# Row maxima stacked under the queries, one ring of four PSUM banks, and one exponential per slot in a vision-transformer block

## The reference

```
gray  = einsum('bchw,c->bhw', x, (0.2989, 0.587, 0.114))
h     = (|conv(gray, scharr_x)| + |conv(gray, scharr_y)|) / 2      # (8, 256, 256): 256 tokens of 256
n     = layernorm(h)
q,k,v = n@Wq+bq, n@Wk+bk, n@Wv+bv        # 16 heads of 16
q,k   = q@Wp, k@Wp                       # per head, 16 x 16
out   = softmax(q k^T / 4) v             # per head, 256 queries by 256 keys
h     = h + out
n2    = layernorm(h)
h     = h + ffn(n2)   # its own layernorm, 256 -> 1024 (silu) -> 256 with dequantised weights, residual + 0.5 z
```

## Time and profile before

| what | value |
|---|---|
| median of 3 runs | 294.59 us |
| the profiled execution | 294.29 us, span 292.6 us, so 1.7 us lie around the span |
| PE busy | 279.8 us (96%), 2336 matmuls |
| DVE busy | 205.7 us (70%) |
| ACT busy | 173.2 us (59%) |
| POOL busy | 145.2 us (50%) |
| mean granted clock of PE | 0.994 |
| DMA packets | 35.9 MB |

### The profile page before, as it was taken

How to read it: one execution, slowest core, us unless ns; L and a number is a source line. 1 busy time by engine, 2 the same in 40 slices (tenths; PEclk the granted TensorE clock), 3 DMA queues, 4 the chain that set the end, 5 groups by cost and what they waited for, 6 DMA issues and landing times.

```text
span 292.6 us, 6337 instructions
## 1 busy us (share of the span) xinstructions
PE 279.8 (96%) x2336; PEld 217.2 (74%) x2336; DVE 205.7 (70%) x394; ACT 173.2 (59%) x330; POOL 145.2 (50%) x286
## 2 busy tenths in 40 slices
PE   4989799999998999999999999999999999999996
PEld 4876678686876676666666665658898999999985
DVE  7659887589988888888998886717926724632323
ACT  2457979766324877777768786686353344444450
POOL 7894387311100129592768655086589399400000
PEclk9999799999999999999999999999999999999999
DMA  6968649998979915676660000000002000100202
GB/s 201 312 193 239 172 165 269 191 275 259 314 217 329 297 43 164 184 208 218 192 157 3 0 2 3 0 3 0 2 0 67 8 0 16 60 0 0 74 0 72
DMA packets 27310, 35.90 MB, mean 123 GB/s; under 512 B 5184, under 2 KB 16272, under 8 KB 27280
## 3 DMA queue, kind: packets, MB, share of 16 engines
q1 hardware_dynamic: 27184, 35.43, 41.4%
q10 hardware_dynamic: 96, 0.07, 0.1%
HBM read 24.42 MB, written 10.49 MB: 119 GB/s over the span
## 4 chain that ended last, share of the span: by engine, by line
PE 70%; DVE 9%; ACT 6%; issue 5%; POOL 4%; DMA 3%; ACTq 1%; SPq 1%; DVEq 0%; POOLq 0%
PE bank L1227 35%; PE bank L1355 9%; PE bank L1307 9%; PE bank L1330 5%; PE bank L1335 4%; DVE negmax L925 4%; PE bank L1373 3%; DMA halo_x<-in_x 2%; PE bank L1365 2%; PE bank L1244 2%; PE bank L1381 1%; ACTq L401 1%; ACT absd L1104 1%; ACT hid L1101 1%; POOL rstd L639 1%
## 5 line engine op out<-in xcount | busy, mean ns | idle before, releaser
L925 DVE TENSOR_REDUCE negmax<-bank 128x2 f32<-128x512 f32 x128 | 82.0, 683 | 6.9 <-PE bank L1307 6.5
L1137 ACT ACTIVATE probs<-bank 128x512 f32<-128x512 f32 x128 | 66.3, 602 | 30.5 <-PE bank L1335 30.5
L979 DVE TENSOR_TENSOR y_l<-yf,y_h 128x512 fp32r<-128x512 f32 x32 | 24.2, 755 | 38.6 <-ACT yf L1163 38.4
L1160 ACT ACTIVATE y_h<-bank,b1col 128x512 fp32r<-128x512 f32 x32 | 22.0, 689 | 47.7 <-PE bank L1227 47.6
L1227 PE MATMUL bank<-w_h,y_h 128*128 128x256 f32 x128 | 36.8, 288 | 0.4 <-DVE osb L987 0.4
L1227 PE MATMUL bank<-w_l,y_h 128*128 128x256 f32 x128 | 36.2, 282 | 0.0
L1227 PE MATMUL bank<-w_h,y_l 128*128 128x256 f32 x128 | 36.1, 282 | 0.0
L1355 PE MATMUL bank<-probs,vals 128*32 128x256 f32 x512 | 34.3, 385 | 0.0
L1307 PE MATMUL bank<-ks,qs 48*128 48x256 f32 x256 | 32.1, 328 | 1.8 <-DVE negmax L925 0.9
L1307 PEld LDWEIGHTS bank<-ks,qs 48*128 48x128 f32 x256 | 19.3, 184 | 15.9 <-DVE negmax L925 7.6
L1330 PE MATMUL bank<-negrow,pick 48*128 48x512 f32 x128 | 26.1, 403 | 0.6 <-DVE pick L1026 0.6
(11 more groups left out here) (164 smaller groups left out, 600.3 us busy)
## 6 DMA issues: line engine op xcount, KB each, us to landing
xr<-in_x SPq DMA_DIRECT2D x8, 768.0 KB, 7.9
qs<-qk_parts SPq DMA_DIRECT2D x48, 128.0 KB, 3.2
ks<-qk_parts SPq DMA_DIRECT2D x48, 128.0 KB, 3.3
qk_parts<-qk_h SPq DMA_DIRECT2D x16, 256.0 KB, 3.1
qk_parts<-qk_l SPq DMA_DIRECT2D x16, 256.0 KB, 3.4
wraw<-in_L_ffn_fc_q SPq DMA_DIRECT2D x4, 512.0 KB, 4.7
wscale<-in_L_ffn_fc_scales SPq DMA_DIRECT2D x4, 512.0 KB, 7.3
out<-osb SPq DMA_DIRECT2D x16, 128.0 KB, 1.8
```

Of the source, the lines that this page charges most:

```text
L925: eng.tensor_reduce(negmax[:, b % 2, u, v], entry_bank(key)[:, :].rearrange("p (t k) -> p t k", t=NT), AX.X, ALU.max, negate=True).then_in ...
L979: eng.tensor_tensor(y_l[:, p % 2, f], yf[:, n % 2], y_h[:, p % 2, f].bitcast(fp32), ALU.subtract).then_inc(s_y, 1)
L1137: eng.activation(probs[:, n % PBUF], p2[n % 4][:, :], ACT.Exp).then_inc(s_exp, 1)
L1160: eng.activation(y_h[:, p % 2, f], src, ACT.Silu, bias=b1col[:, f:f + 1])
```

## The change

1. **Maxima as rows of the stacks.** `STACK = SPLIT + 2` rows are contracted: two rows of `qs` hold the high and the low part of minus the maximum, the same two rows of `ks` hold ones. The matmuls of L1330, `pick` and `picked` go. `negrow` goes to DRAM (`store_max`) and comes back into `qs` by two DMAs (`load_max`), both on SP's queue. The ones are written by DMAs once.
2. **Layout of `qk_parts`**: high and low of a row lie next to each other, so that a half of a pair's stacks is loaded by 8 DMAs instead of 12; the bytes are the same.
3. **One ring of four banks** all through, with the value products as entries of it (`av`). The by-key scores have two buffers of two banks, and one exponential of 1024 columns takes a whole slot (`exp_slot`).
4. **Order**: `AHEAD` 12 instead of 10 (the scores of slots 10 and 11 now belong to the projections of the last pair, those of 8 and 9 stand one step earlier there, and slots 52 to 63 issue no by-query scores); `neg` behind slots 1 and 5 of each eight, `out` behind 3 and 7; so in the steady part every pair of slots has exactly one of the two. The second `neg` of image 0 moves ahead of the slots. GpSimd's weight steps start at slot 6 instead of 10, behind them the other steps at other slots; the second layer's raw weights are fetched at slots 20 and 21 instead of 23 and 24. `OBUF` 7, `PBUF` 12.

```diff
-    AHEAD = 10
+    AHEAD = 12
+    PARTS = 2
+    STACK = SPLIT + PARTS
...
-        NEG_AT = {("qkv", 2, 5): 0}
+        NEG_AT = {("qkv", 2, 5): 0, ("qkv", 3, 3): 1}
         def neg_after(s):
             b, i = s // UNITS, s % UNITS
-            if s == 1:
-                return (0, 1)
-            if i in (3, 7) and b + 1 < B:
+            if s >= 0 and i in (1, 5) and b + 1 < B:
                 return (b + 1, i // 4)
         def out_after(s):
             b, i = s // UNITS - 1, s % UNITS
-            if b >= 0 and i in ((3, 5) if b < B - 1 else (3, 4)):
-                return (b, i // 4 if b == B - 1 else (i - 3) // 2)
+            if b >= 0 and i in ((3, 7) if b < B - 1 else (3, 4)):
+                return (b, i // 4)
...
             if s + AHEAD < SLOTS:
                 head_entries(s + AHEAD)
+            if s % 2 == 1 and 0 <= s - 3 < 2 * GROUPS:
+                entries.append(("av", (s - 3) // 2))
...
             if n < wide:
-                r = n % 4 if n < in_a else n % 3
+                r = n % 4
+            elif key[0] == "av" or key[0] == "out" and key[1] == B - 1 or key[0] == "n3" and key[1] >= 1:
+                r = 0
             else:
-                r = 1 if key == ("n3", 0, 1) else 0
+                r = 1 if key == ("n3", 0, 1) else 3
...
+            def store_max(b, half):
+                eng.wait_ge(s_neg, 2 * b + half + 1)
+                eng.dma_start(neg_dram[b, half], negrow[0:MROWS, half].bitcast(fp32)).then_inc(s_negst[half], 16)
+            def load_max(b, half):
+                r, c = (b // 2) % 2, (b % 2) * N
+                eng.wait_ge(s_negst[half], 16 * (b + 1))
+                for v in range(2):
+                    first = HALF * v + SPLIT
+                    src = neg_dram[b, half, HALF * v:HALF * v + 4 * PARTS].rearrange("(a u) n -> a u n", a=PARTS)
+                    eng.dma_start(qs[first:first + PARTS, r, 4 * half:4 * half + 4, c:c + N].bitcast(fp32), src).then_inc(s_maxrow[half], 16)
...
-            for part in range(4):
+            for part in range(2):
                 load_ffn(0, part)
+            load_max(0, 1)
+            for part in range(2, 4):
+                load_ffn(0, part)
             for s in range(SLOTS):
+                if neg_after(s - 1):
+                    store_max(*neg_after(s - 1))
+                if neg_after(s - 3):
+                    load_max(*neg_after(s - 3))
...
-                if s % UNITS == 1 and b + 1 < B:
-                    split_max(b + 1, 0)
-                if s % UNITS == 5 and b + 1 < B:
-                    split_max(b + 1, 1)
+                if s % UNITS in (0, 4) and b + 1 < B:
+                    split_max(b + 1, s % UNITS // 4)
...
-            def exp_head(n):
+            def exp_slot(s):
...
-                eng.activation(probs[:, n % PBUF], p2[n % 4][:, :], ACT.Exp).then_inc(s_exp, 1)
+                eng.activation(probs[:, n % PBUF:n % PBUF + 2].rearrange("p v n -> p (v n)"), p2[s % 2][:].rearrange("p v n -> p (v n)"),
+                               ACT.Exp).then_inc(s_exp, 1)
...
             def scores_by_key(s):
...
                 if u % 4 == 0:
-                    wait_drained(eng, ("neg", b, u // 4))
+                    eng.wait_ge(s_maxrow[u // 4], 32 * (b + 1))
...
-                for v in range(2):
-                    rows = slice(HALF * v, HALF * v + SPLIT)
-                    eng.matmul(p2[(n + v) % 4][:, :].rearrange("p (t n) -> p t n", t=NT), pick[rows, u % 4:u % 4 + 1].broadcast_to([SPLIT, P]),
-                               negrow[rows, u // 4].unsqueeze(1).broadcast_to([SPLIT, NT, N]), start=True, stop=False)
                 for t in range(NT):
                     for v in range(2):
-                        rows = slice(HALF * v, HALF * v + SPLIT)
-                        ins = eng.matmul(p2[(n + v) % 4][:, t * N:(t + 1) * N], ks[rows, r, u, c + t * P:c + (t + 1) * P],
-                                         qs[rows, r, u, c:c + N], start=False, stop=t == NT - 1)
+                        rows = slice(HALF * v, HALF * v + STACK)
+                        ins = eng.matmul(p2[s % 2][:, v, t * N:(t + 1) * N], ks[rows, r, u, c + t * P:c + (t + 1) * P],
+                                         qs[rows, r, u, c:c + N], start=True, stop=True)
...
                     if G == 0:
                         eng.wait_ge(s_zero, 4)
...
-                    else:
-                        eng.wait_ge(s_ot, G)
+                    wait_room(eng, ("av", G))
```

More of the change, by code:

```diff
@@ L348, in vit_tower_kernel @@
             entries.extend(("n3", p, kf) for kf in range(KE))
-        entry = {key: n for n, key in enumerate(entries)}
-        assert len(entry) == len(entries)
-        drained = {key: n for n, key in enumerate(key for key in entries if key[0] != "neg")}
+        place = {key: n for n, key in enumerate(entries)}
+        assert len(place) == len(entries)
+        entry = {key: n for n, key in enumerate(key for key in entries if key[0] != "av")}
+        drained = {key: n for n, key in enumerate(key for key in entries if key[0] not in ("neg", "av"))}
         ebank, before, held = {}, {}, {}
@@ L372, in wait_drained @@
                 eng.wait_ge(s_neg, 2 * key[1] + key[2] + 1)
+            elif key[0] == "av":
+                eng.wait_ge(s_ot, key[1] + 1)
             else:
@@ L376, in wait_room @@
         def wait_room(eng, *keys):
-            used = sorted((before[key] for key in keys if before[key]), key=lambda key: entry[key])
-            for kind in (True, False):
-                last = [key for key in used if (key[0] == "neg") == kind][-1:]
+            used = sorted((before[key] for key in keys if before[key]), key=lambda key: place[key])
+            for kind in ("neg", "av", None):
+                last = [key for key in used if (key[0] if key[0] in ("neg", "av") else None) == kind][-1:]
                 if last:
@@ L434, in load_qk @@
                 dst = (qs, ks)[op]
-                first = HALF * v + slot
-                src = qk_dram[p, op, part, m * P:(m + 1) * P, :].rearrange("(u v d) t -> v d u t", v=2, d=D)[v]
-                eng.dma_start(dst[first:first + SPLIT - 2:3, r, m * 4:(m + 1) * 4, :].bitcast(fp32), src).then_inc(s_load[r][m], 16)
+                rows = qk_dram[p, op, m * P:(m + 1) * P]
+                if k // 2 % 2 == 0:
+                    first, last = HALF * v, HALF * v + 2 * D
+                    src = rows.rearrange("(u v d) a t -> v (d a) u t", v=2, d=D)[v]
+                else:
+                    first, last = HALF * v + 2 * D, HALF * v + 3 * D
+                    src = rows[:, 1 - op].rearrange("(u v d) t -> v d u t", v=2, d=D)[v]
@@ L487, in _ @@
                 stored(0, m)
-                for k in range(12):
+                for k in range(LOADS):
                     load_qk(0, m, k)
+            stack_ones(0)
             for i in range(4):
```

139 lines of the change are left out of this document (75 added, 64 removed).

## The result

The changed kernel takes **301.59 us** (median of 4 runs, 299.66 to 305.17) against 294.7 us of the kernel before on the same chip: ratio 1.021, 95% interval 1.0135 to 1.0293. It is slower; whether by more than 2% the interval leaves open. Medians here are of all executions, while ratios and their intervals leave out the slow ones, those over 1.5% above the fastest of their kernel (of these four, 305.17). The forecast was 291.4 us with a range of 286.0 to 296.0, so both the sign and the range were wrong. The profiled execution took 300.22 us, its span 298.5 us.

What follows compares the result with a forecast made beforehand. It took the refill loop between PE and VectorE through the four-bank ring as the bound, 3.16 us a pair. Last reduction at 175.0 and last value products at 193.7, 2.9 us earlier, gave 294.3 − 2.9 = 291.4 us, range 286.0 to 296.0.

Steps and rivals of the forecast that it cites:

- PE's load and the steady pair: Attention slots: PE loses 0.23 us in each of 64 slots; the refill loop sets a steady pair at 3.16 us.
- Rival A: Steady pairs: the refill loop does not bind, VectorE's own 2.83 us a pair does; 284.1 us, chance 0.17.
- C: Rival on ScalarE: exponentials of 1.2 us make its pairs 3.2 us and the tail 2.4 longer; 293.8 us, chance 0.11.
- What the change could gain: Slots: by PE's row alone 14.7 us; by the PSUM reading rule alone, only what VectorE idles now.
- Where the slots begin: Start of the slots: heads one step earlier, so slot 12's reductions begin about 1.6 us earlier, at 92.0.
- The maxima's way at the start: Slot 4, image 0: the load of maxima stands behind two 512 KB transfers; PE waits 1.5 us, bounds 0 and 4.7.
- In the steady part two DMAs fit into 11 us: Steady slots: seven slots, 11 us, lie between the maxima's transposition and use, so store and load fit.
- GpSimd's first weight step: Slot 6: it waits for the last weight transfer, ahead of the next maxima's split; 0.3 us, bounds 0 and 1.8.
- Loads two slots sooner: Stack loads: readers come two slots earlier, at least four slots (over 6 us) of cover remain; cost nothing.
- Rival B: SP's queue, image 0, slots 4 and 9: first maxima land late, 4.7 us more; 296.1 us, chance 0.13.
- Rival D: PE's idling lowers the clock to 0.83, its pairs become 3.4 us, 4.4 us more; 295.8 us, chance 0.05.
- Tail: From the last reduction to the start of the last value products: forecast 18.7 us, last value products at 193.7.

Runs made afterwards that it cites:

- e6: The changed kernel without maxima in any form, with the by-query scores refilling the ring by single banks instead of two together: 288.91 us, ratio 0.9792 to the kernel before.
- e4_before_no_max: The kernel before without the 128 matmuls of 512 columns that subtract the maxima; maxima still formed, transposed and copied: 292.6 us, ratio 0.9941.
- e5_no_rows: The changed kernel without the maxima in any form: 48 rows contracted, no rows of ones or maxima, none stored or loaded: 294.71 us, ratio 1.000 to the kernel before.
- e9_direct: The changed kernel with the maxima moved from negrow straight into qs by four 4 KB transfers, without the trip through DRAM: 296.74 us, 5 below the changed kernel.
- e13_early_plain: The changed kernel with direct maxima transfer, early stack loads, feed-forward weights at slots 24 and 25, GpSimd's w1 steps from slot 8: 291.64 us, ratio 0.990 to before.
- e7: The changed kernel with the maxima's store on ScalarE's queue, image 0's second load ahead of the weights, later second-matrix weights and w1 steps: 299.7 us, ratio 1.007 to before.

## Why the prediction was wrong

- *PE's load and the steady pair.* Right: 3.16 forecast, 3.08 to 3.14 measured, for the reason given (0.59 us idle or a division in its place). Rival A did not come, and even with e6's edit a pair takes 3.00, not 2.83. C did not come: the two exponentials of a pair take 1.94 us.
- *What the change could gain.* Right in size (before 13.24 an image, after 12.45). Taking the matmuls away alone brings none of it (e4_before_no_max); what is left to bring it is the ring's order and the division inside the refill. Whether that would come with the 512-wide matmuls kept was not tested: by the prediction's own terms PE would then need 3.04 + 0.46 = 3.50 us in every second pair, more than the 3.16 of the loop.
- *Where the slots begin.* Right: slot 12's heads begin at 91.9, forecast 92.0.
- *The maxima's way at the start.* The step that failed, first half. I gave 1.5 + 0.3 us with bounds 4.7 and 1.8. I placed the wait behind the weights of 512 KB and took SP's own progress from the kernel before. Not seen: `load_max(0, 0)`, placed three DMAs behind its store, holds SP 6.2 us, so that the second store, whose data were ready 9 us before, went out 3 us after the time I had for the first weights. Slot 4 then waited 3.35 us, not 1.5, and the stretch cost 4.6 us over the 12.6 forecast.
- *In the steady part two DMAs fit into 11 us.* The step that failed, second half. I set no duration against the 11 us, though the page had 7.3 us for a transfer in company. Stores of 72 KB took 5.9 and 7.2 us at image 3, in series with SP's order, and slots 39 to 43 took 10.4 us where two pairs were to take 6.3: 4.1 us. The Trainium skill ("DMA: Bandwidth & Descriptors", Anatomy of one DMA) has some 2 us fixed for one DMA issued by GpSimd; an estimate from that page would be 4 us for the two. That is a transfer by itself and of another issuer; the rows here are 3.2 to 7.9 us for the store behind others.
- *GpSimd's first weight step*: I put 0.3 us on it, bound 1.8. It waited 7.8 us in after, under slot 4's lateness. Without that cover a wait of 7.1 us cost some 4.5 (e5_no_rows: slots 19 to 31 in 23.2, at its own 6.22 for four slots 18.7), one of 4.8 us nothing (e9_direct).
- *Loads two slots sooner "cost nothing".* Wrong too, hidden in after: 3.1 us at head 36 when the maxima are punctual (e9_direct).
- *Rival B* named the right place and the right wait, slot 4's, but put it down to the weights ahead of the load; what made it late is the earlier load that held SP. It saw one image; that its 4.7 us are near the 4.6 of image 0 is luck. *Rival D*: in the steady pairs the clock stayed at 1.00 (120 to 130); it fell at the start, for some 1.4 us by e9_direct, and in other runs in the tail, for 1.2 to 1.4.
- *Tail.* 19.05 for 18.7.

Shown by runs: with the direct transfer, the early loads, the later weights and GpSimd's later step, and all else as in after, the kernel comes to the forecast (e13_early_plain). Of the 10 us between, leaving the trip out gives 7 (e5_no_rows), replacing it alone 5 (e9_direct). Open: how the 5 us between e9 and e13 divide between the early loads, the later weights and GpSimd's later step; and why the kernels with the new transfers vary by 3 to 9 us from run to run.

## What to carry to other kernels

An engine busy 99% need not be the bound; look whether the one behind it idles in a closed loop, and take the work away as a test. A new dependent transfer must be costed twice: from issue to landing in the company it will have, and as a wait that holds all that is queued behind it on its queue. When a wait disappears, see what it had covered: here the late maxima had covered GpSimd's wait for its weights and TensorE's wait for the stacks.

## What was not expected of the hardware

- A store of 72 KB took 3.2 to 7.9 us in after while the DMA share was about 1.0 (7.9 for the one issued at 79.39), and 5.5 from ScalarE's queue in e7; where the share was 0.16 it took 1.6 (112.04 to 113.64).
- Rows moved from four partitions to one inside SBUF by four DMAs of 4 KB took 2.4 us of SP's queue to issue, and no trip through DRAM.
- The clock fell in after behind pauses of TensorE of 0.60 and 0.49 us (92.03, 93.02) and stayed at 0.50 from 95 to 105, with TensorE busy 6.65 of 10; in the steady part, with 9.03 of 10, it was 1.00. It fell again in the tail of e13 behind one pause of 1.85 us (0.56 at 176 to 178), and did not in after behind as long a pause (1.00 at 184 to 186).
